# Rows of x reach VectorE's multiplication by DMA through HBM and not by products with spreading matrices; B lies in PSUM; VectorE copies the carry column

## The reference

```python
x_conv = silu(jnp.transpose(xc, (0, 2, 1)))
BC = x_conv @ W_x + b_x
B_mat, C_mat = jnp.split(BC, 2, axis=-1)
A_discrete = jnp.exp(-jnp.exp(A_log))

def step(h, inp):
    xc_t, B_t, C_t = inp
    h = A_discrete[None] * h + xc_t[:, :, None] * B_t[:, None, :]
    y = jnp.einsum('bn,bdn->bd', C_t, h) + D_param * xc_t
    return (h, y)
```

## Time and profile before

| | us |
|---|---|
| median of 3 runs (551.3 to 552.5) | 551.8 |
| profiled execution, its own time | 553.5 |
| its span, first to last instruction | 551.7 |
| TensorE busy | 475.1 (86%) |
| VectorE busy | 403.1 (73%) |
| GpSimd busy | 406.2 (74%) |
| ScalarE busy | 299.0 (54%) |

### The profile page before, as it was taken

How to read it: one execution, slowest core, us unless ns; L and a number is a source line. 1 busy time by engine, 2 the same in 40 slices (tenths; PEclk the granted TensorE clock), 3 DMA queues, 4 the chain that set the end, 5 groups by cost and what they waited for, 6 DMA issues and landing times.

```text
span 551.7 us, 6067 instructions
## 1 busy us (share of the span) xinstructions
PE 475.1 (86%) x1919; PEld 281.5 (51%) x1919; DVE 403.1 (73%) x611; ACT 299.0 (54%) x484; POOL 406.2 (74%) x380
## 2 busy tenths in 40 slices
PE   0786978999998999999989999999989999874765
PEld 0565655754574556555654566455645565331221
DVE  2174043879687978977797888797797769769985
ACT  2664646764666655664675466755556556332120
POOL 1553551998599859995898869995998599848583
PEclk9987979999999999999999999999999999998895
DMA  8400000000000001000100000000100000000000
GB/s 319 165 20 4 1 20 1 1 1 19 1 1 0 1 19 39 1 2 19 40 0 0 21 27 12 1 2 0 40 0 1 0 21 1 0 1 19 0 21 19
DMA packets 5938, 11.83 MB, mean 21 GB/s; under 512 B 912, under 2 KB 1936, under 8 KB 5648
## 3 DMA queue, kind: packets, MB, share of 16 engines
q1 hardware_dynamic: 4752, 9.47, 4.8%
q10 hardware_dynamic: 1152, 1.93, 1.0%
HBM read 9.30 MB, written 2.10 MB: 21 GB/s over the span
## 4 chain that ended last, share of the span: by engine, by line
PE 38%; DVE 25%; POOL 14%; issue 12%; ACT 8%; DMA 2%; SPq 0%; DVEq 0%; ACTq 0%; POOLq 0%
PE bank0a L905 13%; DVE hs L1351 6%; PE bank0a L1018 5%; DVE xbank L1328 5%; POOL hs L522 5%; PE bank1a L985 4%; PE ybank L1054 4%; POOL hidAl L483 4%; DVE plain L1237 3%; DVE beats L1302 3%; DVE beats L1313 2%; PE xbank L1039 2%; DMA Bt<-w_in 2%; POOL xr L503 1%; PE bank1a L970 1%
## 5 line engine op out<-in xcount | busy, mean ns | idle before, releaser
L522 POOL TENSOR_TENSOR hs<-hs,Ct 128x512 f32<-128x512 f32 x127 | 173.2, 1367 | 22.1 <-DVE hs L1351 16.7
L1328 DVE TENSOR_TENSOR xbank<-xbank,Bt 128x512 f32<-128x512 f32 x128 | 88.0, 688 | 27.9 <-PE xbank L1039 27.8
L483 POOL TENSOR_TENSOR hidAl<-plain,hidAh 128x512 fp32r<-128x512 f32 x48 | 68.1, 1420 | 37.9 <-ACT hidAh L617 31.6
L1039 PE MATMUL xbank<-xpair,spr 128*128 128x512 f32 x128 | 69.2, 541 | 22.6 <-DVE hs L1351 22.3
L1351 DVE TENSOR_TENSOR_SCAN hs<-decay,carry,xbank 128x512 f32<-128x512 f32 x63 | 80.6, 1279 | 7.3
L483 POOL TENSOR_TENSOR hidBl<-plain,hidBh 128x512 fp32r<-128x512 f32 x48 | 62.8, 1308 | 29.7 <-ACT hidBh L617 21.9
L1351 DVE TENSOR_TENSOR_SCAN hs<-decay,xbank 128x512 f32<-128x512 f32 x64 | 78.0, 1219 | 5.3 <-DVE xbank L1328 0.5
L616 ACT ACTIVATE plain<-bank0a,col 128x512 f32<-128x512 f32 x64 | 44.1, 688 | 52.3 <-PE bank0a L905 51.2
L1039 PEld LDWEIGHTS xbank<-xpair,spr 128*128 128x128 f32 x128 | 24.4, 191 | 69.1 <-DVE hs L1351 42.8
L905 PE MATMUL bank0a<-hidAh,hTh 128*128 128x512 f32 x128 | 55.5, 434 | 1.4 <-ACT q L649 1.1
L905 PE MATMUL bank0a<-hidBh,hTh 128*128 128x512 f32 x128 | 55.7, 435 | 0.9 <-ACT q L649 0.9
(11 more groups left out here) (187 smaller groups left out, 999.5 us busy)
## 6 DMA issues: line engine op xcount, KB each, us to landing
xt<-x_tok SPq DMA_DIRECT2D x8, 256.0 KB, 2.6
xr<-x_feat SPq DMA_DIRECT2D x8, 256.0 KB, 8.8
out<-xr SPq DMA_DIRECT2D x7, 256.0 KB, 2.0
fh<-h_w SPq DMA_DIRECT2D x1, 1024.0 KB, 11.0
hs<-h_w SPq DMA_DIRECT2D x1, 1024.0 KB, 13.3
lw<-l_w ACTq DMA_DIRECT2D x1, 640.0 KB, 6.4
g<-spread ACTq DMA_DIRECT2D x1, 512.0 KB, 6.3
Bt<-w_in SPq DMA_DIRECT2D x1, 512.0 KB, 8.3
```

The costliest lines, as they stand in the source:

```text
L483: pool.tensor_tensor(low[:, m, :], plain[:, k % NPLAIN, :], high[:, m, :].bitcast(F32), ALU.subtract).then_inc(hidden_low, 1)
L522: pool.tensor_tensor(h, h, Ct[:, hs_(u)], ALU.mult).then_inc(p_ready, 1)
L1039: pe.matmul(xbank[i % 2][:], spr[:, at, :], xpair[:, half, hs_(u)], start=True, stop=True).then_inc(xs_full, 1)
L1328: dve.tensor_tensor(xbank[i % 2][:], xbank[i % 2][:], Bt[:, hs_(u)], ALU.mult).then_inc(xb_ready, 1)
```

## The change

TensorE no longer spreads x. SP stores xc of a unit in a DRAM tensor `x_rows` (two halves in turn), and reads for each step the 8 rows of its group back, each 16 times, into one of `NROWS` = 5 buffers `xs` in SBUF, four steps ahead. VectorE multiplies `xs` by B into a single PSUM bank `xbank`, so that the multiplication of a step waits for the scan of the one before. B is read from `Bt` in SBUF in the first `BSTEPS` = 3 steps and then from `bbank`, a copy in PSUM that ScalarE makes in slot 8 (`keep_B`). `xpair`, `low_x`, the matrices `spr` and their load of 512 KB go. VectorE copies the carry column behind each scan of an even unit, after waiting for that scan, and GpSimd waits for this copy. SP's DMAs are now issued slot by slot.

```diff
+            def keep_x(u):
+
+                sp.wait_ge(l1_act_done, done(L1_ACT, ("conv", u)))
+                if u >= 2:
+                    sp.wait_ge(xb_ready, step(u - 1, 0))
+                sp.dma_start(x_rows[u % 2], xc[:, hs_(u)]).then_inc(x_kept[u % 2], 16)
+
+            def spread_x(u, k):
+                i, g = step(u, k), group_of(k)
+                if k == 0:
+                    sp.wait_ge(x_kept[u % 2], (u // 2 + 1) * 16)
+                if i >= NROWS:
+                    sp.wait_ge(xb_ready, i - NROWS + 1)
+                rows = x_rows[u % 2, DPG * g:DPG * (g + 1), :].rearrange("(o d) t -> o d t", o=1)
+                sp.dma_start(xs[:, i % NROWS, :],
+                             rows.broadcast_to([NSTATE, DPG, HALF])).then_inc(xs_in[i % NROWS], 16)
...
+            def slot(p, s):
+                e, t, n, v, w = units(p)
+                if n is not None and s == 5:
+                    keep_x(n)
+                if n is not None and s == 6:
+                    for k in range(NROWS - 1):
+                        spread_x(n, k)
+                u, k = scanned(p, s)
+                if u is not None and k + NROWS - 1 < NGRP:
+                    spread_x(u, k + NROWS - 1)
+                if s == 6 and 3 <= p + 3 < UNITS:
+                    load_tok(p + 3)
+                if s == 8 and e is not None and e < UNITS - 2:
+                    store(e)
+                if s == 11 and e is not None and e + 4 < UNITS:
+                    load_feat(e + 4)
...
-            for t in range(2, 6):
-                load_tok(t)
-            store(0)
-            load_feat(4)
-            load_tok(6)
-            store(1)
-            load_feat(5)
-            load_tok(7)
-            store(2)
-            load_feat(6)
-            store(3)
-            load_feat(7)
-            for t in range(4, UNITS - 1):
-                store(t)
+            load_tok(2)
+            for p in PERIODS:
+                for s in slots(p):
+                    slot(p, s)
+            store(UNITS - 2)
...
-                pool.wait_ge(xs_done, i + 1)
+                if u % 2 == 0:
+                    pool.wait_ge(carried, u // 2 * NGRP + k + 1)
+                else:
+                    pool.wait_ge(xs_done, i + 1)
...
-                if u % 2 == 0:
-
-                    pool.tensor_copy(carry[:, k:k + 1], h[:, HALF - 1:HALF]).then_inc(carried, 1)
-                    pool.wait_ge(carried, u // 2 * NGRP + k + 1)
                 pool.tensor_tensor(h, h, Ct[:, hs_(u)], ALU.mult).then_inc(p_ready, 1)
...
-                act.wait_ge(l1_act_done, done(L1_ACT, ("conv", t)))
-                for half in range(2):
-                    rows = slice(half * P // 2, (half + 1) * P // 2)
-                    last = act.activation(xpair[rows, half, hs_(t)], xc[rows, hs_(t)], ACT.Copy)
-                last.then_inc(x_high, 1)
...
+            def keep_B(t):
+
+                if t > 0:
+                    act.wait_ge(xb_ready, step(t, 0))
+                act.wait_ge(l1_act_done, done(L1_ACT, ("B", t)))
+                act.activation(bbank[:], Bt[:, hs_(t)], ACT.Copy).then_inc(b_kept, 1)
...
-            act.activation(spr[:].rearrange("p k n -> p (k n)"), raw_spr, ACT.Copy).then_inc(spr_ready, 1)
...
-                def spread_x(u, k):
-                    i = step(u, k)
-                    half, at = divmod(group_of(k), NGRP // 2)
-                    if k == 0:
-                        pe.wait_ge(x_low, u + 1)
-                    if i >= 2:
-                        pe.wait_ge(xs_done, i - 1)
-                    pe.matmul(xbank[i % 2][:], spr[:, at, :], xpair[:, half, hs_(u)], start=True,
-                              stop=True).then_inc(xs_full, 1)
...
-                    u, k = scanned(p, s)
-                    u_next, k_next = scanned(*after(p, s))
-                    if u_next is not None:
-                        spread_x(u_next, k_next)
...
-            def low_x(t):
-
-                dve.wait_ge(x_high, t + 1)
-                for half in range(2):
-                    rows = slice(half * P // 2, (half + 1) * P // 2)
-                    other = slice((1 - half) * P // 2, (2 - half) * P // 2)
-                    last = dve.tensor_tensor(xpair[other, half, hs_(t)], xc[rows, hs_(t)],
-                                             xpair[rows, half, hs_(t)].bitcast(F32), ALU.subtract)
-                last.then_inc(x_low, 1)
...
-                dve.wait_ge(xs_full, i + 1)
-                dve.tensor_tensor(xbank[i % 2][:], xbank[i % 2][:], Bt[:, hs_(u)], ALU.mult).then_inc(xb_ready, 1)
+                elif k == BSTEPS:
+                    dve.wait_ge(b_kept, u + 1)
+                dve.wait_ge(xs_in[i % NROWS], (i // NROWS + 1) * 16)
+                if i > 0:
+                    dve.wait_ge(xs_done, i)
+                b = Bt[:, hs_(u)] if k < BSTEPS else bbank[:]
+                dve.tensor_tensor(xbank[:], xs[:, i % NROWS, :], b, ALU.mult).then_inc(xb_ready, 1)
...
-                dve.tensor_tensor_scan(hs[:, i % NSTATES, :], decay[:, gr:gr + 1].broadcast_to([P, HALF]), xbank[i % 2][:],
+                dve.tensor_tensor_scan(hs[:, i % NSTATES, :], decay[:, gr:gr + 1].broadcast_to([P, HALF]), xbank[:],
                                        0.0 if u % 2 == 0 else carry[:, k:k + 1], ALU.mult, ALU.add).then_inc(xs_done, 1)
+                if u % 2 == 0:
+                    dve.wait_ge(xs_done, i + 1)
+                    dve.tensor_copy(carry[:, k:k + 1], hs[:, i % NSTATES, HALF - 1:HALF]).then_inc(carried, 1)
...
-                    elif s == 6:
-                        low_x(n)
```

More of the change, by code:

```diff
@@ L277, in program @@
         bank1d = ps("bank1d", [P, HALF])
-        xbank = [ps(f"xbank{i}", [P, HALF]) for i in range(2)]
+        bbank = ps("bbank", [P, HALF])
+        xbank = ps("xbank", [P, HALF])
         ybank = ps("ybank", [P, HALF])
@@ L775, in slot @@
                         score_columns(n)
+                        keep_B(n)
                     elif s == 12:
@@ L1484, in constants @@
     n, dd = i // DPG, i % DPG
-    spread = np.zeros((P, NGRP // 2, P), np.float32)
-    for g in range(NGRP // 2):
-        for part in range(2):
-            spread[part * P // 2 + DPG * g + dd, g, i] = 1.0
     gather = np.zeros((P, 2 * P // QUAD - DPG), np.float32)
```

25 lines of the change are left out of this document (12 added, 13 removed).

## The result

The changed kernel takes 545.56 us (median of 5 runs, 542.58 to 547.74) against 551.82 (5 runs): ratio 0.9889, 95% interval 0.9867 to 0.9911. It is 6.3 us faster, and 545.56 lies outside the likeliest case's own range by half a microsecond and inside the whole range. The direction was right, the size was not: 6.3 us came where 16 were forecast.

What follows compares the result with a forecast made beforehand. TensorE with its stalls, racing VectorE, was taken to bound legs G to R; a longer engine chain the legs R to G. Three pairs 12.9, start 1.5, last period 1.5: 16 us less, 536; likeliest range 526 to 545, whole 516 to 552.

Steps and rivals of the forecast that it cites:

- Spread products and stalls go: 16 spread products a unit leave TensorE, with stalls: 3.0 and 2.0 us less per `gate_y`-to-`residual_l0` leg, 0.23 in the others.
- a race between VectorE's own work and TensorE: Leg from G (`gate_y`, slot 9) to R (`residual_l0`, slot 0) set by these two engines: 22.0 us odd, 23.5 even.
- The multiplications with B in SBUF: First three steps read both inputs from SBUF, meeting GpSimd: 0.45 us charged in slot 9, 0.4 in slot 10.
- The carry copies: 64 copies move from GpSimd to VectorE, 0.29 us each there; 0.296 each leave GpSimd.
- rival 2: Carry copy on VectorE waits for GpSimd, 0.53 us more each: 555 us, slower; chance 0.13.
- The pair of units: Two periods: 22.0 + 34.0 + 23.5 + 35.0 = 114.5 us, 4.3 less than 118.8; three pairs 12.9.
- The last period: Spread wait of 3.45 us goes, back-to-back steps 0.22 dearer each: 1.5 us less, bounds 0 and 3.5.
- DMAs priced 0: One store and 16 loads a unit land in time, 5.4 us of slack: price 0 even at doubled landing times.
- The start: 512 KB load of `spread` and first unit's spreads go: 1.5 us less, bounds 0 and 2.5.
- 1 (engines loose): Waits for spreads and copies plus `low_x` come off VectorE whole, carry copies go on: 517.6 us; chance 0.20.
- 3 (shared reads eat the gain): Multiplications from SBUF cost whole GpSimd instructions (1.27 us), slot 8 too: 551 us, no change; chance 0.09.
- The signs that it named: No idle time before multiplications, R's even wait near 0, G's wait 3 us or more, copies 0.15 or less, periods 57.3.

Runs made afterwards that it cites:

- b_direct: Changed kernel, but ScalarE writes B straight into the PSUM bank and all 16 multiplications read it there, no copy of B: 535.89 us.
- early_add: `b_direct` with GpSimd's output addition, ffn product and slot 6 state product put ahead of the hidden remainder it waits for: 523.98 us.
- carry_back: Changed kernel with the carry column copied by GpSimd again, as before the change: 551.48 us.
- spread_load: Changed kernel with the 512 KB of spreading matrices loaded again at the start and rounded by ScalarE, unused: 546.20 us.
- loads_gone: Changed kernel with only the first five `xs` loads issued, the other 123 left out: 543.54 us.
- tail_warm_few: Changed kernel with four extra unread products on TensorE in the last period, where it waits: 543.61 us.
- carry_alone: Kernel before the change, spreads kept, only with the carry column copied by VectorE behind its own scan: 557.41 us.

## Why the prediction missed the size, point by point

- **Spread products and stalls go: right.** No wait for a spread product or for a scan ahead of one is left, and TensorE was off the path in the legs G to R. The estimate for its side, 22.0 and 22.5, could not be seen, because something else ended later.
- **The step that failed: "a race between VectorE's own work and TensorE".** A third engine ran in it. GpSimd's timeline in a leg G to R (G at 385.24, R at 408.18) is busy for 22.86 of 22.94 us:

```profile
389.00 4.59 POOL L548 TENSOR_TENSOR hs<-hs,Ct 128x512 f32<-128x512 f32 x2
393.56 1.75 POOL L492 TENSOR_TENSOR xnTl<-xnT,xnTh 128x512 fp32r<-128x512 f32 x1
395.26 1.30 POOL L510 TENSOR_TENSOR hidAl<-plain,hidAh 128x512 fp32r<-128x512 f32 x1
396.52 1.29 POOL L548 TENSOR_TENSOR hs<-hs,Ct 128x512 f32<-128x512 f32 x1
...
405.27 1.29 POOL L510 TENSOR_TENSOR hidAl<-plain,hidAh 128x512 fp32r<-128x512 f32 x1
406.52 2.53 POOL L548 TENSOR_TENSOR hs<-hs,Ct 128x512 f32<-128x512 f32 x2
```

  It made 22.92 of the odd leg's 22.0. In the legs R to G the 0.23 of the spread product did not come either: `b_direct`, without the meetings, has the 33.80 of the kernel before. That GpSimd kept it is argued from the 0.5 us that `early_add` gains there. The view that would have shown it could be had from the kernel before, windows cut at G and R:

```profile
273.57:298.59 25.02, 22.68 (x98) 14.53 (x98) 20.61 (x20) 16.15 (x26) 23.55 (x17) 1.00 0.00 0
332.39:356.84 24.45, 22.93 (x98) 14.44 (x98) 20.62 (x21) 16.15 (x26) 23.73 (x25) 1.00 0.00 0
```

  GpSimd is busy 23.55 of 25.02 and 23.73 of 24.45 us there, more than TensorE or VectorE, where the earlier trace rows has 84% over the whole periods. A forecast of 22.0 for the odd leg had to say where 1.5 of GpSimd's 23.55 us would go. Part of that time is not work: two products beside VectorE's comparison of 2048 columns (`compare_other`, 3.32 us) took 4.59 us in the rows above, where two alone take 2.53, and four more instructions 1.71 to 1.75 in place of 1.27; that is 3.9 us of the leg, the meetings of the section on B, but with comparisons that both kernels have. `early_add` shows the bound: only GpSimd's order differs from `b_direct`, and the same legs take 21.2 in place of 22.8.
- **The multiplications with B in SBUF: mechanism right, place wrong.** I charged 0.45 in slot 9 and 0.4 in slot 10, and nothing in slot 8, where GpSimd was taken to be idle. It is not: slots 8 and 9 cost 0.45 each, slot 10 0.1, and the first period, which the sum left out, 2.2. From the first to the last R that is 8.6 us where 5.1 (3 x 1.7) were charged.
- **The carry copies: price too high, gain on GpSimd too low.** A copy takes 0.15 us beside a GpSimd that is busy 74% of the span; the rule that the prediction weighed for one column held, and rival 2's extra wait is absent. In the even leg G to R six of them at 0.29 were to make VectorE the bound with 23.5. The leg took 22.92 and VectorE waited 1.26 of it at R, so its side was 21.66. From the start of a scan to the next instruction it is 1.35 us with a copy and 1.14 without, 0.21 for each; and the five comparisons in the leg fell from 8.08 us to 7.36, as GpSimd now more often waits out VectorE than the other way round. The sum gave the copies +1.0 (23.5 for 22.5) and -0.8 a pair; `carry_back` shows -1.5 and -0.9, 2.4 a pair. The -1.5 was missed by the same failed step: GpSimd, whose copies these were, bounds that leg.
- **The pair of units** so came to 116.2 for 114.5: +0.9 and -0.6 in the legs G to R, twice +0.7 in those R to G. Three pairs fell 7.6 where 12.9 were forecast: 5.3 us are missing here, 0.7 in the first period and 3.5 at the end, and the start gave 1.5 too much. That makes the 8.0 by which the profiled executions differ from the forecast; the medians are 1.7 further apart, as the profiled execution before was that much slower than its median.
- **The last period: wrong sign in the profiled execution.** -1.5 was forecast, and it came to +2.0 with the end. Some 2.2 of that is the convolution, 6.5 us for 4.4 at the lower clock, which I had looked for only inside the periods. That the spread products had kept the clock up before is not shown: `spread_load`, `loads_gone` and `b_direct` have none and ran it at 1.00. With the upper level the last leg is 26.83 to 27.23 for 27.38, so -0.2 to -0.5, and -0.5 behind it: less than forecast, too. The wait for the first load of 2.2 us, for which the forecast had 5.4 us of slack, is real in this period, but `tail_warm_few` has it too (2.26) and its last leg is as short as that without loads, 26.83.
- **The start: -3.0 for -1.5, by chance.** At a like clock it is 0.7 at most, and the load of `spread` is worth nothing that can be measured.
- **DMAs priced 0: right in the periods** (`loads_gone`); 0.4 us at most in the last leg, and 0.5 behind it that were not looked into.
- **Rivals.** 1 (engines loose): refuted, G and R hold them together. 2: refuted. 3 (shared reads eat the gain): the mechanism is real and took 8.6 us, half of what was forecast, but not all of it.
- **The signs that it named.** G's waits came (3.36 and 3.46), and so did copies of 0.15. R's wait in even units was 1.26, not near 0, and a period took 58.1, not 57.3. Idle time before the multiplications did not go: the 22.6 us for B took the place of the 27.8 for spreads, one wait for each unit but one.

That `b_direct` takes 535.9, the forecast's 536, is luck: the meetings that it lacks weigh about as much as the GpSimd bound and the ends that the forecast had wrong.

## What to carry to other kernels

Before an edit takes work off the busiest engine, count the busy time of every engine within the leg, not only of the two that wait for each other, and not only over the period: the third (here GpSimd, 84% of the periods and 94 to 97% of the legs G to R) sets how much of the gain is kept. An edit that moves work from GpSimd to VectorE has no price of its own: the same copies gave 5.9 us where GpSimd had the largest share of the chain (40% in `carry_back`) and cost 5.8, in part by the clock, where TensorE and VectorE had it (44% and 34% in `carry_alone`). And before a difference at the start or the end of a kernel is put down to an edit, look at the granted clock there, in several executions. Where VectorE multiplies two operands beside a busy GpSimd, have the producer write one of them straight into PSUM rather than copy it later.
